# Input rows of a two-layer LSTM graph kernel: table rows of 2048 bytes, and x rows of 512 bytes turned and multiplied

## What is computed

```python
def _lstm_last(seq, wih, whh, bih, bhh):          # seq: 33 steps x 512 nodes x 128
    def step(carry, x_t):
        h, c = carry
        g = x_t @ wih.T + h @ whh.T + b
        i, f, gg, o = jnp.split(g, 4, axis=-1)
        c = sigmoid(f) * c + sigmoid(i) * tanh(gg)
        h = sigmoid(o) * tanh(c)
def _sage_conv(x, src, ...):                      # src: 16896 edges = 512 nodes x 33
    msgs = x[src].reshape(n, d, c)
    aggr = _lstm_last(jnp.swapaxes(msgs, 0, 1), ...)
    return aggr @ wl.T + bl + x @ wr.T
h = relu(_sage_conv(x, src, conv1...))
out = _sage_conv(h, src, conv2...)
x = layernorm(x + out)
# then one relational layer: msg = (x @ W[rel])[src] * norm, summed over dst, relu
x = layernorm(x + rgcn(x, ...))
```

## Time and profile before

| | us |
|---|---|
| median of 3 runs (573.68 to 580.67) | 576.14 |
| span of the profiled execution | 570.4 |
| PE busy | 485.2 |
| VectorE busy | 399.5 |
| ScalarE busy | 325.8 |
| GpSimd busy | 309.4 |

### The profile page before, as it was taken

One profiled execution on the slowest core, in us unless ns is written; L12 is line 12 of the kernel. 1 busy time (PEld: TensorE's weight loads), 2 busy tenths in 40 slices (PEclk: granted clock), 3 DMA queues, 4 the chain that ended last, 5 costly groups with the idle time before them and its releaser, 6 DMA issues.

```text
span 570.4 us, 9783 instructions
## 1 busy us (share of the span) xinstructions
PE 485.2 (85%) x3463; PEld 349.4 (61%) x3463; DVE 399.5 (70%) x1114; ACT 325.8 (57%) x832; POOL 309.4 (54%) x320
## 2 busy tenths in 40 slices
PE   8766998979897999778897888887899987978795
PEld 4644786757676785656666766775785543444343
DVE  5544887858676895557776776876787975757665
ACT  4734766737556674545565665655675664545543
POOL 6476565665546501676664566666204655656551
PEclk9997999979999999978989999999999999999899
DMA  5665665675646502665665456556202111111111
GB/s 191 204 188 168 180 192 159 177 195 161 175 125 197 166 11 93 187 180 161 172 169 148 134 163 183 167 169 181 77 1 79 48 38 38 42 38 41 39 42 29
DMA packets 28346, 72.85 MB, mean 128 GB/s; under 512 B 6795, under 2 KB 10691, under 8 KB 28298
## 3 DMA queue, kind: packets, MB, share of 16 engines
q0 software_dynamic: 20768, 64.77, 40.0%
q1 hardware_dynamic: 6442, 6.54, 4.0%
q10 hardware_dynamic: 1088, 0.92, 0.5%
HBM read 69.05 MB, written 3.16 MB: 127 GB/s over the span
## 4 chain that ended last, share of the span: by engine, by line
PE 39%; DVE 17%; ACT 16%; another core or an unknown queue 13%; issue 8%; DMA 6%; POOL 1%; DVEq 0%; ACTq 0%; POOLq 0%
PE gates L1254 18%; DMA edge_rows<-msg_table,msg_index 6%; PE gates L1247 5%; PE work L1254 4%; DVE msg_full L1090 3%; ACT act_if L601 3%; ACT h_hi L597 3%; DVE prod_fc L906 2%; DVE prod_ig L908 2%; ACT msg_full L750 2%; PE work L1247 2%; DVE h_full L877 2%; ACT act_o L619 2%; ACT tanh_c L593 2%
## 5 line engine op out<-in xcount | busy, mean ns | idle before, releaser
L524 POOL DMA_INDIRECT rows<-gate_table,src_steps x226 | 224.7, 994 | 165.1 <-issue 64.5
L1247 PE MATMUL gates<-ident,rows 128*128 128x128 f32 x686 | 99.5, 281 | 39.5 <-issue 20.8
L601 ACT ACTIVATE act_if<-gates 128x512 f32<-128x512 f32 x113 | 67.8, 600 | 104.1 <-remote 54.5
L539 POOL DMA_INDIRECT edge_rows<-msg_table,msg_index x76 | 75.5, 993 | 79.6 <-DMA msg_table<-table_sb 30.9
L1254 PE MATMUL gates<-h_hi,whh_hi 128*128 128x256 f16 x396 | 104.7, 283 | 13.1 <-ACT h_hi L597 6.6
L906 DVE TENSOR_TENSOR prod_fc<-act_if,cell 128x256 f32<-128x256 f32 x128 | 54.2, 424 | 81.3 <-issue 37.3
L1247 PEld LDWEIGHTS gates<-ident,rows 128*128 128x128 f32 x686 | 78.1, 144 | 52.1 <-issue 49.7
L1254 PE MATMUL gates<-h_hi,whh_lo 128*128 128x256 f16 x396 | 104.1, 281 | 0.0
L1254 PE MATMUL gates<-h_lo,whh_hi 128*128 128x256 f16 x396 | 88.1, 282 | 0.4 <-issue 0.4
L890 DVE TENSOR_TENSOR h_lo<-h_full,h_hi 128x256 f16<-128x256 f32 x128 | 54.2, 423 | 12.3 <-ACT h_hi L597 0.9
L1080 DVE TENSOR_SCALAR rows<-node_iota,dst_f 128x512 f16<-128x512 f16 x132 | 43.4, 365 | 26.8 <-ACT msg_full L750 25.7
(11 more groups left out here) (186 smaller groups left out, 800.5 us busy)
## 6 DMA issues: line engine op xcount, KB each, us to landing
rows<-gate_table,src_steps POOLq DMA_INDIRECT x226
gate_table<-rows SPq DMA_DIRECT2D x8, 256.0 KB
edge_rows<-msg_table,msg_index POOLq DMA_INDIRECT x76
code<-code_table SPq DMA_DIRECT2D x6, 160.0 KB
msg_table<-table_sb SPq DMA_DIRECT2D x4, 192.0 KB, 2.4
code<-code_table SPq DMA_DIRECT2D x5, 128.0 KB
whhT<-turned_whh SPq DMA_DIRECT2D x2, 256.0 KB
wihT<-turned_wih ACTq DMA_DIRECT2D x1, 256.0 KB, 2.9
```

Of the source, the lines that this page charges most:

```text
L524: pool.indirect_dma_start(rows[:, j * K + k, :], None, gate_table[l], bass.IndirectOffsetOnAxis(src_steps[:, t, k:k + 1], axis=0)).then_in ...
L539: pool.indirect_dma_start(edge_rows[:, c % 2, n, :], None, msg_rows, bass.IndirectOffsetOnAxis(msg_index[:, pool_first(c) + n:pool_first(c ...
L601: act.activation(act_if[:, h, :], gates[:, h, 0, :], ACT.Sigmoid, scale=1 / G_SCALE).then_inc(if_ready[h], 1)
L1247: pe.matmul(gate_place(t, h, gate)[:, k * P:(k + 1) * P], rows[:, j * K + 2 * h + k, gate * P:(gate + 1) * P], ident[:, :], is_transpose=True,
```

## The change

A table `MODES` gives each step of each layer a way: G is a table step, X an x step, P a one-hot step.

```diff
-WARM = 9
-
-DIRECT = (1, 2, 12)
-HALF = 21
-BY_ONEHOT = (0,) + DIRECT + (HALF,)
-BUILT = (2, 3, 4, 0, 1)
-SPREAD = {1: 3, 2: 4, 4: 0, 5: 1}
+WARM = 18
+
+STEPS = 33
+MODES = ("XXX" + "GXX" * 10, "PP" + "XGX" * 10 + "X")
...
-    DEEP = 5
+    DEEP, XDEEP = 5, 5
+    PICKED = 2
...
+    by_rows, by_x, from_x = steps_of("G"), steps_of("X"), steps_of("XP")
+    fetched = steps_of("GX")
```

```diff
+            issued = [(l, t, k) for l, t in fetched for k in range(K)]
+            for l, t in fetched:
+                if (l, t) == (0, 2):
+                    pool.wait_ge(src_loaded, 16)
+                by_x_row = MODES[l][t] == "X"
+                if by_x_row:
+                    turn = by_x.index((l, t))
+                    if turn >= XDEEP:
+                        pool.wait_ge(rows_turned, 2 * (turn - XDEEP + 1))
+                    if l == 1 and by_x[turn - 1][0] == 0:
+                        pool.wait_ge(h1_stored, 32)
+                else:
+                    turn = by_rows.index((l, t))
+                    if turn == 0 or by_rows[turn - 1][0] != l:
+                        pool.wait_ge(table_stored, 16 * K * (tabled.index(l) + 1))
+                    if turn >= DEEP:
+                        pool.wait_ge(gates1[1], steps_done(*by_rows[turn - DEEP]))
                 for k in range(K):
...
+                    at = issued.index((l, t, k))
+                    if at >= UNDER_WAY:
+                        pool.wait_ge(*landing(*issued[at - UNDER_WAY]))
+                    target, table = ((x_rows[:, x_slot(l, t, k), :], (x, h1_table)[l]) if by_x_row
+                                     else (rows[:, row_slot(l, t, k), :], gate_table[l]))
+                    pool.indirect_dma_start(target, None, table, bass.IndirectOffsetOnAxis(src_steps[:, t, k:k + 1], axis=0)
+                                            ).then_inc(landing(l, t, k)[0], 16)
```

```diff
+            def turn_rows(l, t):
+
+                bank = row_bank[x_turn(l, t) % 2]
+                for k in range(K):
+                    pe.wait_ge(*landing(l, t, k))
+                    to = row_bank[k // 2][:, k % 2 * P:(k % 2 + 1) * P] if (l, t) == (0, 0) else bank[:, k * P:(k + 1) * P]
+                    mm = pe.transpose(to, x_rows[:, x_slot(l, t, k), :], ident[:, :])
+                    if k % 2 == 1:
+                        mm.then_inc(rows_turned, 1)
...
                 for t in range(1, T):
...
+                    input_first, input_second = ((picked_first, picked_second) if of_x(l, t)
+                                                 else (gathered_first, gathered_second))
+                    input_first(t, 0)
+                    input_second(t, 0)
+                    if t + 1 < T and MODES[l][t + 1] == "X":
+                        turn_rows(l, t + 1)
+                    input_first(t, 1)
+                    input_second(t, 1)
                     recurrent(t, 0, l * (T - 1) + t)
...
                     recurrent(t, 1, l * (T - 1) + t)
```

```diff
+                if MODES[l][t] == "X":
+                    act.wait_ge(rows_turned, 2 * (by_x.index((l, t)) + 1))
+                    act.activation(xg_hi[:, i % 2, :], row_bank[i % 2], ACT.Copy, scale=X_SCALE).then_inc(xg_hi_ready, 2)
...
+                if MODES[l][t] == "X":
+                    dve.wait_ge(xg_hi_ready, 2 * (i + 1))
+                    dve.scalar_tensor_tensor(xg_lo[:, i % 2, :], row_bank[i % 2], X_SCALE, xg_hi[:, i % 2, :],
+                                             op0=ALU.mult, op1=ALU.subtract).then_inc(xg_lo_ready, 2)
```

More of the change, by code:

```diff
@@ L63, in build_program, with steps_of, of_x, x_turn @@
     HN = N // 2
-    XS = len(BY_ONEHOT)
-    DEEP = 5
-    SLOTS = DEEP * K
-    fetched = [(l, t) for l in range(2) for t in range(1, T)
-               if t not in DIRECT and (l, t) != (0, HALF)]
-    def gathered_tiles(t):
-        return range(K // 2, K) if t == HALF else range(K)
-    def picked_half(l, t, h):
-        return t in BY_ONEHOT[:-1] or (t == HALF and (l == 0 or h == 0))
-    def picked_nodes(l, e):
-        return slice(0, HN if l == 1 and BY_ONEHOT[e] == HALF else N)
-    def rows_count(turn, k):
-        return sum(k in gathered_tiles(t) for u, (_, t) in enumerate(fetched[:turn + 1]) if u % DEEP == turn % DEEP)
+    DEEP, XDEEP = 5, 5
+    PICKED = 2
+    def steps_of(modes):
+        return [(l, t) for l in range(2) for t in range(T) if MODES[l][t] in modes]
+    by_rows, by_x, from_x = steps_of("G"), steps_of("X"), steps_of("XP")
+    fetched = steps_of("GX")
+    tabled = [l for l in range(2) if "G" in MODES[l]]
+    SLOTS = DEEP * K if by_rows else 12
+    def of_x(l, t):
+        return MODES[l][t] in "XP"
+    def x_turn(l, t):
+        return from_x.index((l, t))
+    def x_slot(l, t, k):
+        return by_x.index((l, t)) % XDEEP * K + k
+    def x_fills(l, t):
+        return by_x.index((l, t)) // XDEEP + 1
+    def row_slot(l, t, k):
+        return by_rows.index((l, t)) % DEEP * K + k
+    def row_fills(l, t):
+        return by_rows.index((l, t)) // DEEP + 1
     TILES = E // P
@@ L310, in build_program @@
         table_stored = sem("table_stored")
-        rows_in = [sem(f"rows_in{s}") for s in range(SLOTS)]
+        landed = [sem(f"landed{s}") for s in range(DEEP * K)]
         gates0 = pair("gates0")
@@ L422, in table_owner, with landing @@
             return 0 if k in (0, 3) else 1
-        def pickings(l, e):
-            return e - 1 if l == 0 else XS - 2 + e + 1
-        def x_part_bank(l, e, part):
-            return pick_pair.get((l, e), (work[:, 0, :], work[:, 1, :]))[part]
+        def landing(l, t, k):
+            turn = fetched.index((l, t))
+            return landed[turn % DEEP * K + k], 16 * (turn // DEEP + 1)
         def steps_done(l, t):
@@ L1221, in _ @@
-            add_bias(0, 1, last=True).then_inc(projected, 1)
-            pe.wait_ge(src_rows_ready, 1)
-            spread_src(2)
-            project(0, xT, 2, first=True)
-            add_bias(0, 2, last=True).then_inc(projected, 1)
+            if 0 in tabled:
+                pe.wait_ge(x_loaded, 16)
+                pe.wait_ge(bias_ready, 2)
+                for k in range(K):
+                    add_bias(0, k, first=True)
+                    project(0, xT, k, last=True).then_inc(projected, 1)
@@ L1226, in _ @@
             pe.wait_ge(ident_ready, 2)
             turn_rows(0, 0)
-            project(0, xT, 3, first=True)
-            add_bias(0, 3, last=True).then_inc(projected, 1)
-            turn_rows(0, 1)
             pe.wait_ge(wih_hi_ready, 1)
@@ L1433, in _ @@
                     pe.wait_ge(residual_ready, K + 1)
+                    pe.matmul(turned_bank[0], ident[:, :], xT_biased[:, 0:HN], start=True, stop=False, skip_group_check=True)
                     for k in range(K):
@@ L1546, in lay_out @@
     steps = arrays["in_src"].reshape(n, -1)
-    laid["direct_rows"] = steps.T[list(BY_ONEHOT)]
+    laid["direct_rows"] = steps.T[0:2]
     laid["step_columns"] = steps.reshape(n // P, P, -1).transpose(1, 2, 0)
```

393 lines of the change are left out of this document (145 added, 248 removed).

## The result

The changed kernel takes 714.06 us (median of 4 runs, 712.17 to 718.81) against 574.94 us before (4 runs, 573.68 to 580.67). The ratio is 1.241, with a 95% interval of 1.232 to 1.250: slower by 24%, where 556 us and at most 600 had been forecast. The profiled execution has a span of 711.7 us, 141.3 more than before.

What follows compares the result with a forecast made beforehand. PE was taken as the bound, busy 85% of 570.4 us, with late completions in steps with gathers. +41 - 65 + 4 + 2 = -18; 570.4 - 18 + 5.7 = 558, taken as 556 us for a shorter first table wait; range 536 to 600.

Steps and rivals of the forecast that it cites:

- PE's work: On PE: 36.5 table steps become x steps, +48; one-hot gathers go, -9.5; their steps' transposes, +2.8; sum +41 us.
- the activations: On ScalarE in x steps: separate biased activations and a copy, 5.61 us, fit under PE's 5.67; friction +4 us.
- GpSimd's pace: On GpSimd: four gathers every step, 256 in place of 234, 1.26 us apart, 1.3 expected with smaller transfers.
- rival 4: ScalarE bounds x steps in its written order at 6.6 us: 593 us, slower; chance 0.12.
- the delayed completions, -65 us: PE's late completions in steps with gathers: 81 us lost now, 16 left as fetched bytes fall; bounds -48 and -81.
- The prediction's own sign of being wrong: "Remote" waits keep their sum, POOL waits for landings at every gather delaying PE's transposes, or PE idles behind ScalarE.
- The 90 us that I had found before: Both layers' long stages before: 53 steps' loss against steps without gathers, about 9 us of it real one-hot work.
- rival 1: PE's completion delay stays at each step, whatever is fetched: 623 us, slower; chance 0.08.
- fast enough: On GpSimd: four gathers take 5.0 us a step against PE's 5.2, so POOL stays just ahead.
- Rival 3: POOL bounds the step at 1.5 us a gather, 6.0 us a step: 576 us; chance 0.26 together with another rival.
- Starts, +2: At the layers' starts: warming matmuls and projection +2; layer 2's bias matmuls and copies +2, lighter gathers -2; together +2 us.
- The rule: DMA against compute engines: by it gathers wouldn't cause the delay, and no part of the 81 us would go.

Runs made afterwards that it cites:

- the paced kernel: Changed kernel with one more GpSimd wait: gathers of step t (above 3) issue only when the gates of step t-3 are done; 611.66 us.
- x rows only: Changed kernel with every step but the two one-hot ones an x step, no table made, stored or gathered; 629.57 us.
- mostly table rows: Changed kernel with table steps for all but the first three steps of each layer; 606.33 us.
- four under way: The kernel with x rows only, with four gathers under way in place of three; 613.31 us.
- one report per x step: Four turned tiles of an x step report once, by two, in place of twice: 721.46 us on the changed kernel, 611.73 us on the paced kernel.
- the shallower rings: Changed kernel with two slots of x rows in place of five and three of table rows in place of five; 651.27 us.
- the one with memsets: The kernel with x rows only, plus a GpSimd memset of 128x192 values behind each gather; 621.46 us.
- two under way: Each gather waits for the landing of the gather two back in place of three: 630.12 us on the changed kernel, 643.49 us on the kernel before.

## Why the prediction was wrong, and where it was right

**Right: PE's work.** Steps of 5.67 and 5.23 us and a table step of 4.80 (4.36 and 0.44) were worked out; 5.71, 5.24 and 4.82 us came. The term of +41 us of PE work came as +38.1 us of busy time in the paced kernel, where the clock stood at 0.97.

**Right: the activations and GpSimd's pace.** ScalarE isn't the bound of an x step (rival 4): the steps at the floor have x steps in them. Gathers of 512 bytes come 1.25 us apart, as I took from the earlier trace rows.

**Wrong: the delayed completions, -65 us.** This is the step that failed. I had found the delay itself in the earlier trace rows, and tied it to the megabyte that a table step fetches, because in the earlier trace rows traffic and loss are there together and away together. But so are GpSimd's gathers, and these the change doesn't lessen: 256 in place of 234. The prediction's own sign of being wrong came: the "remote" waits before the i and f activations, 23.8 us in layer 1's long stage before, are 26.3 there instead of a fifth to a third of that, and 86.8 us in all against 62.0. The 64 steps of both layers took 392.4 us before and take 528.8 us now. Of these 136.4 us more, 41 are PE's work, and the rest, about 95, is what stands in the place of the -65. (Above the quiet floor of 5.26 us the changed kernel's 64 steps lose 528.8 - 64 x 5.26 = 192 us. The 90 us that I had found before cover 53 steps; all 64 lose 392.4 - 64 x 4.48 = 106 us, work of the one-hot steps included.) Pacing alone takes 102 us away again: in the paced kernel the 64 steps take 422.4 us, 30.0 more than before, which is 11 less than PE's added work.

**Wrong: the bounds of this term.** I gave nothing as its upper end (rival 1, 623 us) and so took for granted that the loss per step cannot grow. With pacing it didn't: 611.66 us, near rival 1's sum. What made it grow was an edit that I had not priced at all: two rings of five steps in place of one. With x rows only there is one ring of five, and 84 of the changed kernel's us are gone (629.57). With two, GpSimd can be eight steps ahead, and it is let go again by the turning of an x step five x steps back. PE turns rows in two steps of three, so GpSimd gets 8 to 12 gathers at once, holds PE's completions for that long, and then has to wait until PE has caught up (10.07 us in the turn shown). My sum treated GpSimd as fast enough (5.0 us against 5.2 us a step) and stopped there; it should have asked in what portions it issues, and what happens on PE meanwhile. Rival 3 had GpSimd as the bound of a step, by late landings; with x rows only GpSimd's four gathers do set the step (6.17 us), but by PE's late release.

**Starts, +2.** Steps 1 to 4 of both layers take 61.5 us more, nearly all of it part of the 95 above. I had counted PE's and the copies' work there, and not the 36 gathers that GpSimd issues in a row.

**The rule.** The Trainium skill, "SBUF — State Buffer", section "Who interferes with whom", has it that DMA never contends with a compute engine. With the stall at 47 GB/s and the steady step of 6.2 us for rows of 512 and of 2048 bytes, the runs agree that bytes aren't what PE waits for. I had set the rule against the loss as a whole, and that didn't follow: gathers can hold PE's completions back without the bytes of their data being the cause.

**Why the kernel before is hard to beat.** Four gathers in a row and one late release, 6.2 us, is what a step with gathers cost in these runs, whatever stood in the row: 6.17 and 6.22 us measured. The kernel before already stands near it with 5.82 us a step, steps without gathers among them. Cutting bytes alone didn't help it; fewer gathers shortened a step (5.71 us with three of four, 5.45 without those of most x rows), though neither of these kernels gives the reference's output, and with their starts neither was faster as a whole (597.49 against 585.98, 616.16 against 582.87). No version tried here is faster than the kernel before beside it. Of those with the reference's output the nearest are the changed code with mostly table rows (23 us behind), x rows only with four under way (27) and the paced kernel (41, and 23 with one report per x step); one run each can't rank these.

## What to carry to other kernels

When a queue issues indirect gathers beside matmuls that others wait for, count gathers and look at their unbroken runs before counting bytes. A deeper ring is not free cover: it lets the queue run longer in one go, and a release that comes in big portions turns into stalls as long as these. If two things in a trace come and go together (here traffic and gathers), price the change once for each of them, and let a loss also grow in the bounds.

## What was unexpected in the hardware

- PE's completions, and only these, come late while GpSimd issues gathers in a row: in the changed kernel some 110 events of PE's semaphores come over 2 us after the last recorded matmul that counts them, and some 70 in the kernel before; of ScalarE's and VectorE's none does in either before the last 0.3 us of the program. This is counted over all events of semaphores that one engine alone counts up.
- The hold mostly begins 3 to 5 us into a run, at its third or fourth gather, and ends about 0.8 to 2 us after the last of a run of four to twelve. Some event of PE's is overdue for 1 to 3 us in most runs of four, 5 to 8 in runs of eight, and in runs of twelve 10 to 15 in the changed kernel and 6 to 11 with the shallower rings.
- It doesn't go with bytes, nor with three or four under way, nor with the number of completions. Why PE's completions and GpSimd's issue get in each other's way stays open; the traces show the times and not the path, and no run separates GpSimd's own work on a gather from the packets that the gather makes. Open too are why the completions within a stall come about one per gather, and why the kernel before and the one with memsets pass through long runs with shorter stalls.
- With two under way, the table gathers of a step came 1.8 us apart in the median in the kernel before, and it took 643.49 us against 570.69: there the pauses for landings cost more than the hold that they avoid, while the changed kernel gained 84 us by them.
